# A cross-attention kernel: the two spreading products of a batch are issued behind its attention products instead of ahead of them

## The reference

```python
x = x + xattn(layernorm(x), ctx_1024, mask, Wq, bq, Wkv, bkv, Wo, bo)   # 16 heads of 32, rotary on q and k
x = x + attn(layernorm(x), c_attn_kernel, ..., c_proj_kernel, ...)      # causal self-attention, 16 heads of 32
x = x + ffn(layernorm(x), gate_w, gate_b, expert_w, expert_b)           # 8 experts, the best 2 of each token
```

```python
q = layernorm(x) @ Wq + bq;  k, v = split(context @ Wkv + bkv)          # context: 257 rows of 512
scores = einsum('bhqd,bhkd->bhqk', larope(q), larope(k)) * SCALE        # 16 heads x 32 queries x 257 keys
attn = softmax(where(mask, scores, -inf));  out = einsum('bhqk,bhkd->bhqd', attn, v)
return out @ Wo + bo
```

## Time and profile before

| | |
|---|---|
| median of 3 executions | 793.52 us (792.46 to 793.53) |
| the profiled execution | 790.52 us, span 788.7 us |
| mean granted TensorE clock | 0.985 of full |
| TensorE matmul busy | 767.9 us, 97% |
| TensorE weight load busy | 647.7 us, 82% |
| VectorE / ScalarE / GpSimd busy | 489.8 / 340.4 / 216.2 us |

### The profile page before, as it was taken

How to read it: one execution, slowest core, us unless ns; L and a number is a source line. 1 busy time by engine, 2 the same in 40 slices (tenths; PEclk the granted TensorE clock), 3 DMA queues, 4 the chain that set the end, 5 groups by cost and what they waited for, 6 DMA issues and landing times. The chain is left out here.

```text
span 788.7 us, 21576 instructions
## 1 busy us (share of the span) xinstructions
PE 767.9 (97%) x9062; PEld 647.7 (82%) x9063; DVE 489.8 (62%) x1130; ACT 340.4 (43%) x816; POOL 216.2 (27%) x192
## 2 busy tenths in 40 slices
PE   8999999999999999999999999999899999699997
PEld 7888888888888888888889888898677777578884
DVE  6656565565656556656465655857789998822236
ACT  5533544334453344533445334544556674123330
POOL 0222223222233222332222322222123321146640
PEclk9999999999999999999999999999999999889999
DMA  8722001100011000110000101111753227645548
GB/s 298 271 80 89 28 29 50 34 28 30 28 39 44 29 29 29 36 48 28 29 28 28 55 28 30 41 69 55 295 228 140 115 95 276 263 136 171 182 130 315
DMA packets 22445, 78.11 MB, mean 99 GB/s; under 512 B 3248, under 2 KB 3760, under 8 KB 19408
## 3 DMA queue, kind: packets, MB, share of 16 engines
q1 hardware_dynamic: 18528, 64.45, 22.4%
q0 software_dynamic: 3680, 12.06, 4.7%
q10 hardware_dynamic: 144, 0.26, 0.1%
HBM read 58.15 MB, written 18.61 MB: 97 GB/s over the span
## 5 line engine op out<-in xcount | busy, mean ns | idle before, releaser
L161 PE MATMUL bank<-chi,wparts 128*128 128x258 f32 x496 | 143.7, 290 | 0.0
L163 PE MATMUL bank<-chi,wparts 128*128 128x258 f32 x496 | 140.1, 282 | 0.0
L162 PE MATMUL bank<-clo,wparts 128*128 128x258 f32 x496 | 140.0, 282 | 0.0
L334 POOL TENSOR_TENSOR pdiag_hi<-p_last_and_rinv_hi,const 128x256 fp32r<-128x256 f32 x32 | 19.7, 617 | 328.4 <-DVE p_last_and_rinv_hi L581 328.4
L328 POOL TENSOR_TENSOR ksin<-kb,const 128x1032 f32<-128x1032 f32 x32 | 95.0, 2969 | 41.7 <-ACT kb L381 41.7
L786 PE MATMUL bank<-wparts,chi 128*128 128x512 f32 x256 | 105.7, 413 | 0.0
L161 PEld LDWEIGHTS bank<-chi,wparts 128*128 128x128 f32 x496 | 93.5, 189 | 12.8 <-issue 12.8
L787 PE MATMUL bank<-wparts,chi 128*128 128x512 f32 x256 | 101.5, 397 | 0.0
L788 PE MATMUL bank<-wparts,clo 128*128 128x512 f32 x256 | 101.1, 395 | 0.0
L373 ACT ACTIVATE chi<-craw 128x1032 fp32r<-128x1032 f32 x32 | 34.2, 1069 | 146.3 <-PE bank L788 144.2
L557 DVE TENSOR_TENSOR v<-bank,bias_cross 128x512 f32<-128x512 f32 x64 | 43.9, 688 | 83.9 <-PE bank L788 83.9
(11 more groups left out here) (335 smaller groups left out, 1684.5 us busy)
## 6 DMA issues: line engine op xcount, KB each, us to landing
craw<-ctx_t_dram SPq DMA_DIRECT2D x32, 516.0 KB, 3.4
expert_lo<-weights_dram SPq DMA_DIRECT2D x8, 1024.0 KB, 13.2
expert_hi_scratch<-wraw SPq DMA_DIRECT2D x16, 512.0 KB, 2.9
wparts<-expert_hi_scratch SPq DMA_DIRECT2D x8, 1024.0 KB, 9.5
wraw<-weights_dram SPq DMA_DIRECT2D x7, 1024.0 KB, 5.6
expert_lo<-ffn_out_scratch SPq DMA_DIRECT2D x16, 256.0 KB, 5.4
x<-x_dram SPq DMA_DIRECT2D x8, 256.0 KB, 7.7
out_dram<-x SPq DMA_DIRECT2D x8, 256.0 KB, 2.2
```

The source lines that it names most:

```text
L161: pe.matmul(psum, ahi(c), bhi(c), start=(c == 0), stop=False)
L162: pe.matmul(psum, ahi(c), blo(c), start=False, stop=False)
L163: last = pe.matmul(psum, alo(c), bhi(c), start=False, stop=(c == chunks - 1))
```

## The change

On TensorE the two spreading products of batch b come behind its attention products. VectorE's `o_sum` waits for them as well.

```diff
                 def o_sum(b):
 
                     dve.wait_ge(s_av, b + 1)
+                    dve.wait_ge(s_spread, b + 1)
                     if at_start(b):
                         dve.wait_ge(s_vlsb, 2)
@@
                             q_transposed(t + 1, b)
                         if more:
                             v_product(b + 1, j + 1, 1)
+                        attend(b, j)
                         diagonals_spread(b)
-                        attend(b, j)
```

## The result

The changed kernel took 797.83 us in the median of 6 executions (796.22 to 799.66), the kernel before 792.97 us on the same chip (791.73 to 793.53). The ratio is 1.0062, 95% interval 1.0044 to 1.008: slower by 4.9 us (3.5 to 6.3), a small loss but one clear of the scatter. The forecast was 6.2 us slower. The profiled execution of the changed kernel has a span of 794.4 us, against 788.7.

The account below looks back on a forecast made before the run. TensorE's list was taken to bound the cross-attention stage; 0.20 us more per batch at its borders, 31 times, gave 6.2 us, so 793.5 + 6.2 = 799.7 us (+0.8%), chance 0.76, range 796.0 to 802.2 us.

Parts of the forecast that it names:

- What bounds the stage: Cross-attention stage: TensorE's list sets the end, busy 65.00 of 65.00 us, so its loss of 0.20 us per batch reaches the end.
- The borders: Last v matmul to next scores' first load: changes of array piece cost some 0.1 us each; 1.25 us becomes 1.44.
- rival 4: Full array into 32x32 pieces at its upper bound: 0.31 us lost per batch, 9.6 us slower, 803.1 us; chance 0.06.
- The term that was mis-sized: the scores: Scores on 32x32 pieces, from their first load on: as long as before, 1.45 us.
- rival 3: Scores run faster as instruction supply catches up: up to 0.52 us won per batch, in full 783.6 us; chance 0.04.
- the sign: Distance between two batches' scores must grow by 0.2 us, or the prediction is wrong.
- Rival 1: Load of `same` hidden behind the strips, only drains paid: 0.10 us per batch, 3.1 us slower, 796.6 us; chance 0.09.
- Rival 2: Leaving strips for the full array is free: 0.03 us in place of 0.13 + 0.10, no change, 793.2 us; chance 0.05.
- The covers: Moved products and VectorE's new wait cause no waiting: some 5 us of cover for attention products, VectorE idle 1.5 us per batch.
- The size in the median: Whole kernel: median taken 3.0 us above the profiled execution, so 793.5 + 6.2 = 799.7 us.

Follow-up runs that it names:

- one_more_border: Kernel before, plus one unread full-array matmul of 32 columns between attention products and next scores: 798.64 us against 793.26, ratio 1.0076.
- bf16_after_full: Changed kernel's order, with the spread's high and low parts, diagonals and `same` in bfloat16, on the full array: 791.58 us against 789.31 for the kernel before.
- wait_only: Kernel before with only VectorE's new wait for the spread added, TensorE's order kept: 793.45 us against 793.26, ratio 1.0002.
- bf16_before_full: Kernel before, its order kept, with the spread's parts and `same` in bfloat16 on the full array: 793.54 us against 793.34, ratio 0.9998.
- bf16_after_strips: Changed kernel's order, spread's parts and `same` in bfloat16, spreading on four 128x32 strips: 788.41 us against 789.31 for the kernel before, ratio 0.9976.
- spread_amid: Kernel before with the spreading products moved into the middle of the attention products: 801.0 us against 793.26, ratio 1.01.

## Why the prediction was right

**What bounds the stage.** Right. The trace names no wait of TensorE between 48 and 540 us in the changed kernel either, and the measured loss (4.9 us, 3.5 to 6.3) is what the stage's distances give (5.26 and 5.07 us).

**The borders.** Right, term by term. Expected and found between the last v matmul and the scores' first load: 0.32 and 0.32; 0.57 + 0.13 and 0.69; 0.22 and 0.23 between the two spreading matmuls; 0.20 and 0.20 out of the full array into 32x32 pieces, the one border that the trace of before did not have behind 256 columns. The sum came out at 1.44, as reckoned; in the medians over the batches it is 1.452 against 1.255 before, so this stretch grew by the forecast 0.20. The upper bound of the border into 32x32 pieces (rival 4) had counted the wait for ScalarE's copy as border.

**The term that was mis-sized: the scores.** I let them take 1.45 us from their first load on, as before. They take 1.43 in the changed kernel and in one_more_border. The first scores of the kernel before had shown the same 1.43; I had noted 0.02 "to win" under rival 3 and left it out of the sum. The 0.02 lies at the entry: behind the 64 attention products the first load starts at 310.83 and the first matmul 0.03 later, while in the changed kernel both start at 326.93; what follows, up to the key product, is 0.01 longer there.

```profile
310.86 0.37 PE L802 MATMUL bank<-kcos,qt 32*32 32x257 f32 x1
```

So two batches' scores moved apart by 0.18 us, not by the 0.20 that I had named as the sign; the 0.02 is 0.6 us of the difference between the forecast 6.2 and the measured 5.26. Another 0.2 is that the stage as measured holds 30 of the 31 trips, and 0.15 is the one stop that the trace of before has ahead of batch 23.

**The rivals.** Rival 1 (the load of `same` hidden) falls: 0.23 between the two spreading matmuls. bf16_after_full, where the load is hardly exposed, is near 2 us slower, where I had put 3.1 for a hidden load. Rival 2 (leaving the strips is free) falls with 0.69 in place of 0.60, and one_more_border prices the round trip. Rival 3 (faster scores through supply) had the right sign and a twenty-fifth of the size. Both the 0.03 at the entry and the stops are gone where another product stands between the attention products and the scores, even one matmul of 32 columns (one_more_border). That is the direction of its mechanism, but at the entry and not within the scores. No run tests supply itself, and the last scores of the kernel before start their load and their first matmul together, at 539.00, though they follow 64 attention products too. The cause stays open. Rival 4 falls.

**The covers.** Right: no wait of TensorE at the attention products or the scores, none of VectorE at line 591. wait_only shows it by itself.

**The size in the median.** The forecast of 799.7 us stood on a median of 793.5; six executions put the kernel before at 793.0, which is 0.5 of the 1.9 us between forecast and measurement. Before batch 1 and behind batch 31 single executions differ by several us, so a single pair of profiled spans (5.7 us apart here) agreed with the timed difference partly by luck. The second trace of the changed kernel has a span of 792.6 us, only 3.9 above that of before, with the same stage.

## What to carry to other kernels

When matmuls on pieces of the array of different shape stand in one list, count the borders and not the matmuls. Here the trip from the strips to the full array with float32r weights cost 0.18 us per batch, as much for one matmul of 32 columns as for the pair of 256, and a small product placed within a run of its own shape cost only its columns. If a product must stand beside strips, give it the strips' shape (shown here in bfloat16 alone), or at least weights whose load is short. And read such costs from start to start: the share of busy time was 97% in both kernels.

## What the runs showed of the hardware that I had not expected

- The load exposed on entering the full array depends on the type: the second matmul of 256 columns starts 0.23 us behind the first in float32r, 0.12 in bfloat16, where within the full array it is 0.12 in both (float32r in the kernel before, bfloat16 in bf16_before_full).
- Attention products in float32 and spreading products in bfloat16 ran on the strips without any stop between them; a change of type is no border (324.94 us for both, in bf16_after_strips).
- The scores on 32x32 pieces take 0.02 us less from their first load on (1.43 in place of 1.45) when the 64 attention products do not stand directly ahead of them (the last scores of a kernel are an exception). The shape ahead of them is not what decides: in bf16_after_strips and in nearly all batches of spread_amid strips stand ahead of them, and they take 1.43.
- A list that is never named as waiting can still stop: up to 0.16 us at single entries from attention products into scores, in the traces of the six kernels that have them side by side, and in none of the five traces where another product stands between.
